# Adaptive-norm attention and expert block: scores from 16-bit halves against f32 scores on row tiles, with all weights laid out beforehand

## The reference

```python
h    = relu(x @ (down * dg + db)) @ (up * ug + ub) + x   # dg, db, ug, ub = cond @ gamma/beta, 64 hidden
p    = sigmoid(h @ Wp + bp)                              # 8 heads, 5 levels each
sim  = cumprod(pq * pk + (1 - pq) * (1 - pk)).sum() / 5  # per pair of tokens and head
x1   = x + softmax(causal(sim)) @ (h @ Wv) @ Wo          # 8 heads of 32 features
y    = x1 @ weight + bias                                # weight, bias = ((cond @ W_dec + b_dec) as (257, 30)) @ V
out  = x1 + y + expert[argmax(y @ gate)] @ y             # 8 experts of 256 x 256
```

## Time and profile before

| | |
|---|---|
| median of 3 runs | 181.53 us (181.46 to 181.69) |
| span of the profiled execution | 181.9 us |
| PE, PEld busy | 157.2 us (86%), 97.4 us |
| DVE, ACT, POOL busy | 108.7, 79.2, 44.8 us |
| transfers | 20.38 MB in 14745 packets |

### The profile page before, as it was taken

One profiled execution on the slowest core, in us unless ns is written; L12 is line 12 of the kernel. 1 busy time (PEld: TensorE's weight loads), 2 busy tenths in 40 slices (PEclk: granted clock), 3 DMA queues, 4 the chain that ended last, 5 costly groups with the idle time before them and its releaser, 6 DMA issues.

```text
span 181.9 us, 3567 instructions
## 1 busy us (share of the span) xinstructions
PE 157.2 (86%) x1399; PEld 97.4 (54%) x1399; DVE 108.7 (60%) x200; ACT 79.2 (44%) x126; POOL 44.8 (25%) x83
## 2 busy tenths in 40 slices
PE   0796876998889999989999999939999948998784
PEld 0535643446555655546575666617656616675563
DVE  2433584327278839698938469972856792483521
ACT  2001480237786464696364447833433553411010
POOL 8700000002110202310731212093212175052020
PEclk9999978999999999999999999996999996999999
DMA  5999996782208760004870000287210000001101
GB/s 155 226 459 377 320 297 163 166 227 57 34 13 206 181 182 0 5 0 93 205 170 29 29 29 32 64 190 170 74 43 18 29 4 2 29 4 58 58 29 58
DMA packets 14745, 20.38 MB, mean 112 GB/s; under 512 B 3536, under 2 KB 10364, under 8 KB 14600
## 3 DMA queue, kind: packets, MB, share of 16 engines
q1 hardware_dynamic: 13672, 19.25, 37.7%
q0 software_dynamic: 336, 0.45, 1.3%
q10 hardware_dynamic: 720, 0.46, 0.9%
HBM read 9.54 MB, written 2.22 MB: 65 GB/s over the span
## 4 chain that ended last, share of the span: by engine, by line
PE 64%; DVE 13%; issue 8%; POOL 6%; ACT 4%; DMA 2%; POOLq 0%; SPq 0%; ACTq 0%; DVEq 0%
PE work L639 28%; PE s_ps L639 17%; PE c_ps L639 13%; POOL zo L387 5%; DVE rden L478 5%; DMA x_nat<-in_x 2%; PE work L841 2%; DVE feat L630 2%; DVE h_t L521 1%; PE work L760 1%; ACT prob L410 1%; DVE pick L613 1%; POOL prob L379 1%; PE work L726 1%; ACT x_t L414 1%
## 5 line engine op out<-in xcount | busy, mean ns | idle before, releaser
L410 ACT ACTIVATE prob<-s_ps 128x1024 f32<-128x1024 f32 (+1 forms) x48 | 42.0, 881 | 32.9 <-PE s_ps L639 32.6
L379 POOL TENSOR_SCALAR_AFFINE_SELECT prob<-prob 128x512 f32<-128x512 f32 x32 | 21.3, 666 | 117.8 <-ACT prob L410 117.8
L478 DVE RECIPROCAL rden<-c_ps 128x256 f32<-128x256 f32 x16 | 28.1, 1755 | 8.9 <-PE c_ps L639 8.9
L639 PE MATMUL s_ps<-st 128*128 128x256 f16 (+1 forms) x192 | 26.3, 260 | 0.2 <-DVE q_bd L544 0.2
L639 PEld LDWEIGHTS s_ps<-st 128*128 128x128 f16 x192 | 13.6, 98 | 17.4 <-issue 14.5
L639 PE MATMUL c_ps<-prob,v_two 128*32 128x256 f32 (+1 forms) x288 | 20.6, 355 | 2.1 <-POOL prob L379 2.1
L594 DVE TENSOR_TENSOR wdec<-wdec,prob 128x1024 f32<-128x1024 f32 (+1 forms) x16 | 16.9, 1059 | 4.9 <-POOL prob L379 4.5
L387 POOL TENSOR_TENSOR zo<-z_nat,pick 128x256 f32<-128x256 f32 x16 | 16.5, 1053 | 11.6 <-DVE pick L613 11.3
L639 PE MATMUL work<-wo,ctx_t 128*128 128x256 f32 x64 | 18.8, 420 | 0.0
L639 PE MATMUL work<-gexp,wdec 128*128 128x256 f32 x64 | 17.7, 402 | 0.0
L619 DVE TENSOR_TENSOR x_nat<-work,x_nat 128x256 f32<-128x256 f32 x16 | 6.7, 421 | 16.9 <-PE work L639 16.9
(11 more groups left out here) (135 smaller groups left out, 206.5 us busy)
## 6 DMA issues: line engine op xcount, KB each, us to landing
st<-feat_h SPq DMA_DIRECT2D x64, 128.0 KB, 2.4
wdec<-in_L_cond_W_dec SPq DMA_DIRECT2D x1, 3855.0 KB, 18.5
x_nat<-in_x SPq DMA_DIRECT2D x4, 512.0 KB, 4.1
ex_nat<-in_L_ffn_expert_w SPq DMA_DIRECT2D x1, 2048.0 KB, 23.7
out_x<-x_nat SPq DMA_DIRECT2D x16, 128.0 KB, 1.7
w_vl<-in_L_attn_Wv SPq DMA_DIRECT2D x1, 256.0 KB, 4.7
wo<-in_L_attn_Wo POOLq DMA_DIRECT2D x1, 256.0 KB, 11.7
gam_up<-in_L_cond_up_gamma ACTq DMA_DIRECT2D x1, 128.0 KB, 2.1
```

The source lines that it names most:

```text
L379: nc.gpsimd.affine_select(out=tri, in_=tri, compare_op=ALU.is_ge, fill=0.0, base=0, pattern=[[0, HG], [1, P]], channel_multiplier=-1).then ...
L410: nc.scalar.activation(prob[:, u % RING, :, 0:n], s_ps[:, u % 2, :, 0:n], ACT.Exp).then_inc(exped, 1)
L478: link(nc.vector.reciprocal(rden[:], c_ps[m % 2][:, CW:2 * CW]))
L639: return nc.tensor.matmul(o, w, r, start=start, stop=stop, skip_group_check=True)
```

## The change

The changed program computes the same function with another layout and another list.

- **Input layout.** The host hands over seven arrays: x transposed, the experts transposed, W_dec, and four packed ones, in which Wo, V and the gate stand in both layouts where needed. The output leaves transposed (features on partitions). The transposes of x, experts, Wo, V and gate leave TensorE, and their copies leave ScalarE and VectorE. All loads are issued by SyncE.
- **Scores.** The halves, their copies and the 64 stacking transfers are gone. The transposed features (4 heads x 32 on 128 partitions) are scaled once in f32 (`phi_t`), and each head's scores are an f32 matmul with a contraction of 32, on the row tile (32 rows of the array) of its own; four heads fill four banks.
- **Pairs.** Two units make a pair: 24 pairs, one exp and one mask per pair. `s_ps` is now one buffer of four banks (before: two), `prob` has two.
- **Column tiles.** V, gate-up, the outputs, `Wo U`, Q and z's transposes are written as four matmuls of 32 output partitions each (`tiled`).
- **Keys' sums.** Of the short chunks the half with two key blocks is added on GpSimd (`short`), so TensorE multiplies 2 x 128 columns with ones instead of 256 + 128. Long chunks add on VectorE as before, with the two blocks of a pair at once.
- **Order.** The prologue prepares sequence 0 alone; sequence 1's V, the rest of W_dec and the experts come in the gaps of sequence 0. The last sequence's `zo` is made by VectorE, and its output is five pieces, the last two of 128 columns.

```diff
-            def scores(u):
-                b, (g, kt, q0, n, _, _) = unit(u)
-                if u % BU == 0:
-                    pe.wait_ge(stacked[b], 16 * 4 * HG)
-                if u >= 2:
-                    pe.wait_ge(exped, u - 1)
...
-                for h in range(HG):
-                    ins = mm(s_ps[:, u % 2, h, 0:n],
-                             st[:, b % 2, g, h, P * kt:P * (kt + 1)], st[:, b % 2, g, h, T + q0:T + q0 + n])
+            def tiled(o, w, r, start, stop):
+                for j in range(P // DH):
+                    part = slice(DH * j, DH * (j + 1))
+                    ins = mm(o[part], w[:, part], r, start=start, stop=stop)
+                return ins
+            def scores(p):
+                b, (g, _, units, _, first, _) = pair(p)
...
+                    pe.wait_ge(exped, p)
...
+                for i, (kt, q0, n) in enumerate(units):
+                    for h in range(HG):
+                        rows = slice(NF * h, NF * (h + 1))
+                        ins = mm(s_ps[:, h, CW * i:CW * i + n], phi_t[rows, b % 2, g, P * kt:P * (kt + 1)],
+                                 phi_t[rows, b % 2, g, q0:q0 + n])
+                if not half:
+                    for h in range(HG):
+                        mm(den[DH * h:DH * (h + 1), 0:P], ones[:], prob[:, p % 2, h, 0:P], start=False, stop=True)
+                    pe.wait_ge(mixed, mixes(p))
+                    for h in range(HG):
+                        ins = mm(den[DH * h:DH * (h + 1), P:CW], ones[:], short[:, mixes(p) % 2, h, :], start=False, stop=True)
...
+                    pool.wait_ge(exped, p + 1)
+                    nc.gpsimd.affine_select(out=tri, in_=tri, compare_op=ALU.is_ge, fill=0.0, base=0,
+                                            pattern=[[0, HG], [0, 2], [1, P]], channel_multiplier=-1
...
+                        nc.gpsimd.tensor_tensor(short[:, mixes(p) % 2], both[:, :, 0, P:CW], both[:, :, 1, 0:P], ALU.add
...
+PROLOGUE = [("gdn", (0,)), ("gdn", (1, 2, 3)), ("gup", 0), ("ugR",), ("down", 0), ("ugT",), ("up", 0, 0), ("up", 0, 1), ("gup", 1),
+            ("VL", 0, 0), ("VL", 0, 1), *features(0, FIRST), ("feat", 0, FIRST), ("VL", 0, 2), ("VL", 0, 3),
+            *features(0, SECOND), ("down", 1), ("phi", 0, 0, FIRST), ("phi", 0, 1, FIRST), ("U", 0), ("scores", 0),
```

More of the change, by code:

```diff
@@ L27 @@
 U_PIECE = U_COLS // 4
[L31 to L35, removed]
-BC = 2 * NG
[L37 to L48, removed]
@@ L51, in chunks @@
[L51 to L76, removed]
-ALL_T, FIRST, SECOND = (0, 1, 2, 3), (0, 1), (2, 3)
[L82 to L87, removed]
@@ new lines, in mixing, with mixes, masks, opening @@
+def mixing(p):
+    return pair(p)[1][1] == 0
+SHORT = [p for p in range(ALL) if mixing(p)]
+def mixes(p):
+    return sum(mixing(i) for i in range(p + 1))
+def masks(p):
+    return sum(pair(i)[1][3] for i in range(p + 1))
+def opening(p):
+    return pair(p)[1][1] == 1 and pair(p)[1][4]
+def long(p):
+    return pair(p)[1][1] == 1
+def adds(p):
+    return sum((1 if opening(i) else 2) for i in range(p + 1) if long(i))
+ALL_T, FIRST, SECOND = (0, 1, 2, 3), (0, 1), (2, 3)
+def part(b, ts):
+    return 1 if ts == FIRST else b + 2
@@ L128, in between @@
     if b == B - 1:
-        gaps[7] += [("zT", b, FIRST)]
-        gaps[8] += [("zs", b, FIRST), ("zo", b, 0)]
-        gaps[11] += [("out", prv, 3), ("zoT", b, 0)]
-    return gaps
-ORDER = PROLOGUE + [("eT", 2), ("eT", 3)]
-_open = []
+        gaps[2] += [("zT", b, FIRST)]
+        gaps[5] = [("out", prv, 2), ("zoT", b, 0), ("close", ALL - 1), ("out", prv, 3)]
+    return gaps
+ORDER = list(PROLOGUE)
 for _b in range(B):
[L138 to L149, removed]
+    for _i, (_a, _c) in enumerate(zip(after_scores(_b), after_context(_b))):
+        _p = _b * BP + _i
+        if _p + 1 < ALL:
+            ORDER += [("scores", _p + 1)]
+        ORDER += _a
+        ORDER += [("context", _p)]
+        ORDER += _c
+        if _p + 1 < ALL and long(_p + 1):
+            ORDER += [("add", _p + 1)]
@@ L157, in build @@
-def build(nc, x, cond, down_project, down_gamma, down_beta, up_project, up_gamma, up_beta, Wp, bp, Wv, Wo,
-          W_dec, b_dec, V, gate_w, expert_w, out):
+EARLY_TURNS = [sum(k == i for k in EARLY_BANK.values()) for i in range(EARLY)]
+def build(nc, x_tr, first, lift, vl, mix, W_dec, expert_tr, out_tr):
     with ExitStack() as ctx:
@@ L704, in _ @@
                     continue
+                if s == ("gup", 0):
+                    for _ in range(1):
+                        mm(c_ps[0][:, 0:P], zeros[:], zeros[:])
                 _, k, turn = WORK[s]
```

850 lines of the change are left out of this document (457 added, 393 removed).

## The result

The changed kernel takes 138.18 us (median of 6 runs, 137.84 to 138.64), the kernel before 181.94 us in the same set of runs; the ratio is 0.7593, with a 95% interval of 0.7559 to 0.7626. Forecast were 146 us, 134 to 161, faster.

What follows compares the result with a forecast made beforehand. TensorE was taken to bound the list between a prologue chain and a tail chain. Prologue 18, TensorE's work 101, waits 13 and tail 14 summed to 146 us, range 134 to 161.

Steps and rivals of the forecast that it cites:

- rival D: Waits in TensorE's list: GpSimd's adds are quick and waits fall to 4 us, total 137 us; D and better, chance 0.17.
- Row tiles at 0.44 a unit: Scores: four heads on four row tiles run at once, so a unit of 256 columns costs one f32 product, 0.44 us.
- A's weight loads: Scores: row tiles' weight loads pass one after another, 0.88 us a unit, 25 us more, total 171; chance 0.09.
- B's price: Scores: the four heads don't overlap at all, 40 x 1.32 = 53 us more, total 199; chance 0.03.
- The term for a change: TensorE's list: each change of tiling between neighbouring groups costs 0.11 us; 62 changes make 6.8 us.
- TensorE's work, 101 us: List from first scores to last denominators: priced products, transposes and changes of tiling sum to 101 us, before 108.5.
- The waits, 13 us: TensorE's list: five kinds of waits and slow clock add 13 us, with bounds of 4 and 28.
- The short sums (1): Short chunks: TensorE waits for mask and GpSimd's add, 3.1 us after exp; 5 us over 8 pairs.
- the long ones (2): Long chunks: sums close 3.5 us after the exp, partly covered by TensorE's work; 4 us over 7.
- `zo` (4): GpSimd's four products at 1.05 us, 4.2 in all, delay the fourth pair's mask; 2 us over two sequences.
- the clock (5): TensorE's list: slow clock after the waits costs 1 us.
- Rival C's bubble: Single scores buffer and longer exp leave a 0.5 us bubble in each of 24 pairs, total 158; chance 0.2.

Runs made afterwards that it cites:

- same_rows: Changed kernel with all four heads' scores read from the first head's rows, one row tile: 197.9 and 198.3 us in two runs, 201.8 and 207.0 in the others.
- full_width: Changed kernel with the products written as four column tiles made one full-width product again: 144.08 us.
- short_twice: Changed kernel with each short sum on GpSimd made a second time into a tile nobody reads: 140.95 us.
- v1_first: Changed kernel with sequence 1's up and V put ahead of the first scores instead of in the gaps: 142.60 us.
- before_layout: Kernel before with only x and the experts arriving transposed, their 64 transposes and 16 copies gone: 179.31 us, ratio 0.9807.
- sums_f16: Changed kernel with the last addition of the keys' sums written as f16, their product with ones one record: 134.61 us, ratio 0.7389.
- heads_in_turn: Changed kernel with scores ordered head by head, both units of a head together, instead of unit by unit: 138.27 us.

## Why the prediction was right, and where it was not

- **The number.** 138.2 us lies inside 134 to 161, but outside the band of 141 to 152 that had half the chance; it is rival D's, with 0.17. In spans the miss is 9.7 (146 against 136.3): the waits were put 12.7 too high, prologue and tail 0.9, and TensorE's work 3.9 too low (104.9 against 101). That the last cancels part of the first is luck.
- **The bound and the three parts.** TensorE bounds the list, right. Prologue 17.2 (18.0) and tail 13.9 (14) came as forecast, the list at 105.2 for 114.
- **Row tiles at 0.44 a unit.** Right (0.43). Rivals A and B are out by the changed kernel's rows (A's weight loads take 0.18 us each, but all 16 of a pair are done in 0.74), and `same_rows` shows that B's price was sized rightly: 60 us with its clock against 52. The ratio of 3.07 in the Trainium skill, "TensorE: Matmul & The Clock Gate", section "Measured speedup vs the span model", is for one pack of 512 columns. Here a whole pair of 256 and 128 columns goes 2.81 / 0.87 = 3.2 times as fast as on one row tile, near it, but within a pair four records go in the time of one (0.21): the shortfall stands once per group of scores, not in each unit, so it cost 24 x 0.11 = 2.6 us and not the 5 that follow from 0.57 a unit.
- **Narrow products stream no faster.** Right (0.43 to 0.45); what they save is 6.0 us, by `full_width`. The term for a change was mis-sized for wide blocks: 0.18 for one between narrow groups, not 0.11.
- **TensorE's work, 101 us.** Nearly right: 105.2 elapsed with 0.3 idle, so 3.9 us are in the prices. The term that was mis-sized is the changes of tiling around scores, 48 at 0.11: each of the 24 groups costs 0.33, not 0.22, which is 2.6 of the 3.9. What makes the first records of a group slower was not tried. (A block of 8 transposes takes 1.02, not 0.88 + 0.11, which is little.)
- **The waits, 13 us.** This is the step that failed: 0.3 us of idle time. The short sums (1) and the long ones (2) were priced as if TensorE stood at the exp's end, (1) with 3.1 us from there against what followed it. In the trace TensorE is later than that by 0.3 to 3.4 us in every pair, with its own work. In the first pair the exp ends at 19.62 and the next scores start at 20.37, so 0.75 of the 1.3 us forecast there were this lateness. The rest was price: the short sum stood 2.5 us after the exp, not 3.1, since it took 1.28 and not 1.7. Of the other waits, `zo` (4) took 0.61 each instead of 1.05, and the clock (5) stayed at 1.00. Rival C's bubble in each pair is not there either, since no scores come sooner than 0.27 us after the exp before them. Rival D, with waits of 4, gave 137, and was the better forecast; its reason (quick adds) was only half of it, since `short_twice`, where GpSimd takes 2.56 for each sum, is still at 141.
- **Prologue.** Right within 0.8; down started at 7.04 for 7.0. That the program keeps what the prologue loses is shown for a part only: putting 5 us of work back costs 4.5 (`v1_first`), and the transposes of x and the experts are worth 3.6 in all (`before_layout`). What the stacking transfers and the rest of sequence 1's work cost there was not tried.
- **Clock.** In the sum as 1 us of new slow clock; there was none. The kernel before had slow stretches (0.94 in one stage), and that they are the rest of 2.7 us in the list is argued, not shown by an experiment.

## What to carry to other kernels

Small f32 products with a contraction of 32 are worth trying on four row tiles with a bank for each: here the unit cost one product, and halves, stacking and their transfers were saved. Count the changes of tiling in the built order (here 0.1 each, 0.2 for a wide block among narrow ones, 0.3 in all around a group of scores) and write neighbours in one form. Price a wait from where the waiting engine really stands, pair by pair; when the bound engine is always late, side work on other engines is free up to that slack, and work taken from it shows nearly in full (3.5 of 3.9 us in `sums_f16`).

## What the runs showed of the hardware

- Records of different row tiles pass each other in TensorE's queue: with two products of one head side by side a pair still took 0.89 us, against 0.86 (`heads_in_turn`, with the rows above).
- GpSimd's product of 256 elements took 0.6 us alone and about 1.5 beside VectorE's additions of two operands in SBUF. In the kernel before, two of them alone, and two beside additions:

```profile
173.83 1.19 POOL L387 TENSOR_TENSOR zo<-z_nat,pick 128x256 f32<-128x256 f32 x2 [9.14 <-DVE pick L613]
```
```profile
119.24 3.08 POOL L387 TENSOR_TENSOR zo<-z_nat,pick 128x256 f32<-128x256 f32 x2
```
```profile
119.08 1.21 DVE L594 TENSOR_TENSOR wdec<-prob 128x1024 f32<-128x1024 f32 x1
120.42 1.42 DVE L594 TENSOR_TENSOR wdec<-wdec,prob 128x1024 f32<-128x1024 f32 x1
```

  and in the changed one four of them took 2.33 us in each of three sequences, most of it beside a reciprocal that reads PSUM:

```profile
53.20 2.33 POOL L433 TENSOR_TENSOR zo<-z_nat,pick 128x256 f32<-128x256 f32 x4 [4.14 <-DVE pick L649]
```
```profile
53.69 1.76 DVE L520 RECIPROCAL rden<-c_ps 128x256 f32<-128x256 f32 x1 [0.57 <-PE c_ps L687]
```

  The Trainium skill, "GPSIMD Engine Reference", section "1. Specifications", names this contention: GpSimd shares its interfaces to SBUF with VectorE, and they contend when VectorE's instruction has two inputs in SBUF. The traces agree. By these rows it made 1.9 of the wait of 2.12 in the earlier trace rows (3.08 against 1.19, an estimate), and `zo` now stands beside the reciprocal, which fits its lower price; no run moved it to try this.
- Scores on one row tile in turn held TensorE busy all the time (60.00 of 60.00 us) and still went with a granted clock of 0.91 from 60 to 120 us, and of 0.50 from 64.30 to 65.60 (`same_rows`).
